# The output bias moves from GpSimd to VectorE and to a late place; the scatters of rows are no longer tied to TensorE's progress

## The chip, the cores and the metric

One core of one Trainium2 chip. The metric is the device time of one execution in microseconds (us), lower is better; before the change it is the median of three runs.

## The reference, cut to what matters

```python
x = L0_attn_x                               # (4, 512, 256) float32
xn = _layernorm(x, axis=-1)
# attention: 16 query heads of 16, one key/value head, window of 64, rotary on 8 of 16 dims
out = softmax(rope(q) . rope(k) * scale + mask) @ v
attn = out @ Wo + bo                        # bo: the output bias, one row of 256
# mixture of experts: 64 experts, 4 per token, 64 hidden, and two shared experts of 256
comb = top-4 gates of softmax(flat @ router_w), chosen with router_bias
routed = einsum('ne,nef,efd->nd', comb, silu(flat @ wg) * (flat @ wu), wd)
shared = sum over s of (silu(flat @ swg[s]) * (flat @ swu[s])) @ swd[s]
return x + attn + routed + shared
```

## The kernel before

The 2048 tokens are 16 tiles (NT) of 128; four tiles make one of the four batches (TPB = 4, B = 4). All five engines run hand-written streams side by side and meet at semaphores. On each engine the order in which the program issues is the order of execution.

**Start.** x is loaded (`x_in`, in the upper part of the tile `wall`), normalised into `x_n` (tile `spare`), turned on TensorE into `xnT`, and projected. The router runs on VectorE as a generator `routing()` whose steps are put between other work; it yields `slot_i`, for each token and each of its four experts the row of the DRAM buffer `xs_d` where its copy has to go (semaphore `slots`, L1229, once for tiles 0 to 7 and once for 8 to 15).

**Attention, 16 turns.** Turn T of every engine handles several tiles at different steps: TensorE computes the maxima of the scores of tile T (L459), the scores of T-1 (L487), the weighted values of T-1 (L530), the output projection of T-2 (L555). VectorE reduces the maxima (L1109), makes the parts of the float32 queries that bf16 leaves over (`leave`, L1103, two operands in SBUF), splits the maxima (L1118, L1120) and lays out the keys (`near`, L1095); `add_x` (L1154) adds x to the projected attention and SyncE stores the result in `base_d`.

**GpSimd in these turns.** `rotate(T)` applies the rotary embedding to the queries of a tile in four instructions (L1501 to L1507). `scatter()` issues 64 indirect DMAs (L1517, one for each tile and expert place), each writing 128 rows of 1 KB into `xs_d`. `add_bias(b)` (L1574) adds `bo` to the four tiles of `x_in` of batch b, so that `add_x` brings the bias along; it was loaded as one of the first DMAs into `bo_sb`. The order on GpSimd is: rotations 0 to 4 and the keys, the eight additions of batches 0 and 1, then a loop over T (L1597) that issues `SCATTERED_AT(T)` scatters, four or six, each after a wait for a product of TensorE in turn T, and after each of them one instruction of `rotate(T + 4)` or of `add_bias`.

**The blocks of experts.** When all 64 scatters have landed, SyncE loads blocks of 128 sorted rows (`xrow`, L1732), TensorE turns them (L639), and 32 groups (NGRP) of up to four blocks run: gate and up product (L665), `silu` on ScalarE (L913), the product of both on VectorE (`hidden`, L1301), the down product (L690), the copies out (L925, L1308) and the store to `y_d`. For each block GpSimd copies the weights of the expert that the router chose out of the resident tables (`pick_weights`, L1544, and `pick_down`, L1563). In groups 24 to 27 SyncE loads `base_d` back into `acc` (L1812, one DMA for each batch).

**The end.** The shared experts (L604, L889, L1315, L1319, L624), `add_shared` (L1326) into `acc`, and `sum_up` (L1341), which adds the four gathered rows of each token with their gates; GpSimd gathers them with 64 indirect DMAs (L1634).

## Time and profile before

| | |
|---|---|
| median of 3 runs | 394.87 us (392.55 to 395.25) |
| the profiled execution | 395.41 us, of which the span from first to last instruction is 394.1 us |
| TensorE busy | 345.3 us (88%) |
| GpSimd busy | 259.9 us (66%) |
| VectorE busy | 250.0 us (63%) |
| ScalarE busy | 189.1 us (48%) |
| mean granted TensorE clock | 0.961 of full speed |

Busy shares are means over stages with different limits: the start (to about 34 us), the attention (to about 172 us), the groups of experts (to about 290 us) and the shared experts with the sums (to the end).

### The profile page before, as it was taken

What the parts mean: (1) busy time and instruction counts of PE and PEld (TensorE: products, weight loads), DVE (VectorE), ACT (ScalarE), POOL (GpSimd) and SP (SyncE); (2) the same over time, 40 slices, a digit from 0 to 9 for tenths busy, and PEclk for the clock granted to TensorE, in tenths of its full rate; (3) what the DMA queues carried; (4) which work ended last, traced back from release to release, by engine and by line L of the source; (5) the groups of instructions that cost most, each with busy time, mean ns of one, the idle gap of its engine ahead of it and who ended that gap; (6) DMA issues with size and microseconds to landing.
All of it is one profiled execution on the core that took longest, in us unless ns stands there. A gap on an engine that the chain in (4) does not pass through costs nothing.

```text
span 394.1 us, 8678 instructions
## 1 busy us (share of the span) xinstructions
PE 345.3 (88%) x2710; PEld 254.8 (65%) x2711; DVE 250.0 (63%) x717; ACT 189.1 (48%) x359; POOL 259.9 (66%) x522
## 2 busy tenths in 40 slices
PE   6788597998888886999999999999999998899463
PEld 3676465666656554588999999999855544454352
DVE  4878797879889975555555544444443266581956
ACT  2684676788887873454555545545421010100100
POOL 5568988777687876326566667778647757575740
PEclk9999689899999998999999999999999999999958
DMA  8940245355665545779988845688753424343431
GB/s 253 220 122 3 81 129 158 123 163 162 175 182 166 187 150 162 198 215 292 298 258 268 258 146 176 205 279 277 270 180 105 118 80 133 90 142 90 119 108 40
DMA packets 73036, 66.81 MB, mean 170 GB/s; under 512 B 9053, under 2 KB 68701, under 8 KB 72993
## 3 DMA queue, kind: packets, MB, share of 16 engines
q1 hardware_dynamic: 66433, 49.30, 42.1%
q0 software_dynamic: 6144, 16.79, 13.6%
q8 instruction: 23, 0.38, 0.4%
q10 hardware_dynamic: 416, 0.18, 0.3%
q14 instruction: 20, 0.16, 0.1%
HBM read 36.78 MB, written 29.23 MB: 167 GB/s over the span
## 4 chain that ended last, share of the span: by engine, by line
PE 54%; DVE 18%; another core or an unknown queue 11%; issue 8%; ACT 7%; DMA 1%; POOL 1%; DVEq 0%; SPq 0%; ACTq 0%; POOLq 0%
PE bank L665 14%; PE bank L690 9%; PE bank L604 4%; PE bank L639 4%; DVE xall L1341 4%; PE bank L530 3%; PE bank L555 3%; PE bank L418 3%; DVE xall L1109 3%; PE bank L624 3%; PE bank L437 2%; PE bank L487 2%; ACT xall L855 2%; PE bank L406 2%
## 5 line engine op out<-in xcount | busy, mean ns | idle before, releaser
L1634 POOL DMA_INDIRECT wall<-y_d,y_row x64 | 60.9, 952 | 35.0 <-issue 18.3
L1517 POOL DMA_INDIRECT xs_d<-spare,slot_i x64 | 64.7, 1011 | 24.8 <-PE bank L487 6.3
L665 PE MATMUL bank<-xall,spare 128*128 x508 | 63.8, 278 | 0.0
L1301 DVE TENSOR_TENSOR spare<-bank,spare 64x512 f32<-64x512 f32 (+1 forms) x64 | 44.1, 689 | 31.0 <-ACT spare L913 30.2
L1544 POOL COPY spare<-wall 128x256 f32 x127 | 48.4, 400 | 19.4 <-PE bank L665 9.6
L665 PEld LDWEIGHTS bank<-xall,spare 128*128 128x128 f32 x508 | 59.4, 192 | 2.1
L604 PE MATMUL bank<-xnT,xall 128*128 128x512 f32 x128 | 58.3, 596 | 0.6 <-issue 0.3
L925 ACT ACTIVATE spare<-bank 128x512 f32<-128x512 f32 (+1 forms) x62 | 33.7, 593 | 27.9 <-PE bank L690 17.7
L624 PE MATMUL bank<-xall 128*128 128x256 f32 x128 | 33.2, 410 | 12.7 <-DVE xall L1326 8.7
L889 ACT ACTIVATE xall<-bank 128x512 f32<-128x512 f32 x16 | 9.2, 596 | 68.9 <-remote 51.6
L864 ACT ACTIVATE xall<-bank 98x1024 bf16<-98x1024 bf16 x32 | 32.7, 1023 | 19.9 <-PE bank L437 12.0
L604 PEld LDWEIGHTS bank<-xnT,xall 128*128 128x128 f32 x128 | 23.9, 190 | 26.9 <-issue 26.1
L624 PEld LDWEIGHTS bank<-xall 128*128 128x128 f32 x128 | 25.9, 206 | 23.6 <-DVE xall L1326 11.0
L872 ACT ACTIVATE xall<-bank 128x512 f32<-128x512 f32 x64 | 36.3, 600 | 7.5 <-PE bank L487 5.7
L1341 DVE SCALAR_TENSOR_TENSOR xall<-wall,gate,xall 128x256 f32<-128x256 f32 x64 | 31.0, 486 | 2.3
L913 ACT ACTIVATE spare<-bank 64x512 f32<-64x512 f32 (+1 forms) x32 | 18.8, 588 | 26.2 <-PE bank L665 26.1
L1109 DVE TENSOR_REDUCE xall<-bank 128x4 f32<-128x316 f32 x64 | 28.1, 477 | 2.4 <-remote 1.8
L855 ACT ACTIVATE xall<-xall 128x768 bf16<-128x768 f32 (+2 forms) x48 | 28.9, 626 | 1.1 <-DVE xall L1103 0.7
L1171 DVE COPY xall<-bank 128x256 f32<-128x256 f32 x32 | 13.6, 424 | 24.5 <-PE bank L639 24.1
L487 PE MATMUL bank<-xall,wdn 128*128 128x256 bf16 x120 | 21.9, 287 | 7.5 <-ACT xall L872 3.4
L1326 DVE TENSOR_TENSOR xall<-xall,bank 128x256 f32<-128x256 f32 x16 | 6.6, 417 | 25.8 <-remote 15.6
L1563 POOL COPY small<-wdn 128x128 f32 x24 | 7.0, 293 | 22.0 <-PE bank L690 21.3
(174 smaller groups left out, 648.8 us busy)
## 6 DMA issues: line engine op xcount, KB each, us to landing
y_d<-spare SPq DMA_DIRECT2D x31, 512.0 KB, 3.7
wall<-in_wg SPq DMA_DIRECT2D x16, 256.0 KB, 4.8
wall<-in_wu SPq DMA_DIRECT2D x16, 256.0 KB, 4.9
wdn<-in_wd SPq DMA_DIRECT2D x16, 256.0 KB, 4.4
spare<-xs_d SPq DMA_DIRECT2D x32, 128.0 KB, 2.9
small<-xs_d SPq DMA_DIRECT2D x32, 128.0 KB, 3.1
wall<-in_x SPq DMA_DIRECT2D x4, 512.0 KB, 5.6
base_d<-spare SPq DMA_DIRECT2D x16, 128.0 KB
```

What stands on the lines that cost most here:

```text
L604: ins = pe.matmul((gate_bank(i), up_bank(i))[half], wsh[:, c, half, ex, f0:f0 + P], xnT[:, c, g * GN:(g + 1) * GN], start=c == 0, stop=c = ...
L624: ins = pe.matmul(shared_bank(T), hs[T // GT % 2][:, k, t * P:(t + 1) * P], wshd[:, k, :], start=k == 0, stop=k == FC - 1)
L665: ins = pe.matmul(up_bank_of(G)[:, j * P:(j + 1) * P], wcur[i % NW][:, c * 2 * F:(c + 1) * 2 * F], x_half[c][:, bass.ds(o, P)], start=c == ...
L690: ins = pe.matmul(o[:, j * P:(j + 1) * P], hT[G % 2][rows64, j * P:(j + 1) * P], down_weights_of(G)[j][rows64, :], start=True, stop=True)
L855: act.activation(qt[:, :, first:first + n, :], source.unsqueeze(2).to_broadcast([P, H, n, HD]), ACT.Copy).then_inc(s["q_part"], 1)
L872: act.activation(probs[n % 2][:, e * 512:(e + 1) * 512], bank[2 + e][:, :], ACT.Exp).then_inc(s["exp"], 1)
L1109: dve.tensor_reduce(maxf[T % 2][:, w * 8 + 4 * e:w * 8 + 4 * e + 4], bank[e][:, 0:4 * NEAR].rearrange("p (g n) -> p g n", g=4), AX.X, ALU.max,
L1301: ins = dve.tensor_tensor(hT[G % 2][half, 0:n], up_bank_of(G)[F:P, 0:n], sg[0:F, 0:n], ALU.mult)
L1341: dve.scalar_tensor_tensor(a, yk[:, T, k, :], gate[:, T, k:k + 1], a, ALU.mult, ALU.add).then_inc(s["sum"], 1)
L1517: pool.indirect_dma_start(out=xs_d, out_offset=bass.IndirectOffsetOnAxis(ap=slot_i[:, T, k:k + 1], axis=0), in_=x_n[b][:, t, :], in_offset ...
L1544: pool.tensor_copy(wcur[i % NW].rearrange("p (c g f) -> p c g f", c=NC, g=2), wall[:, bass.ds(o, WE)].rearrange("p (g c f) -> p c g f", c= ...
L1634: pool.indirect_dma_start(out=yk[:, T, k, :], out_offset=None, in_=of, in_offset=bass.IndirectOffsetOnAxis(ap=y_row[:, T, k:k + 1], axis=0 ...
```

## The change

The bias is no longer added on GpSimd. VectorE adds it to `acc`, one instruction of 128 x 1024 elements for each batch, in groups 28 to 31, and `bo` is loaded in group 18. Later readers of `acc` wait for `with_bo`. On GpSimd the scatters wait for nothing but `slots`; turn 0 issues eight of them, turns 1, 12 and 13 five, the others four. Where no instruction of a rotation is there to stand between two scatters, a `memset` of 128 x 1 does. In `rotate`, the wait for the second instruction stands now behind the next scatter, in front of the third instruction.

```diff
+    bo_late = xrow[2]
-    SCATTERED_AT = lambda T: 6 if T in (NT - 4, NT - 3) else 4
+    BIAS_AT = 18
+    SCATTERED_AT = lambda T: 8 if T == 0 else 5 if T in (1, NT - 4, NT - 3) else 4
...
         def add_x(T):
             dve.wait_ge(s["attended"], T + 1)
-            dve.wait_ge(s["x_bo"], T + 1)
...
+        def add_bias(b):                       # VectorE
+            dve.wait_ge(s["bo"], 16)
+            dve.wait_ge(s[f"acc{b}"], 16)
+            a = acc[:, b * TPB:(b + 1) * TPB, :]
+            dve.tensor_tensor(a, a, bo_late.unsqueeze(1).to_broadcast([P, TPB, D]), ALU.add).then_inc(s["with_bo"], 1)
...
         for G in range(1, NGRP + 1):           # VectorE, the groups
             ...
             for b in turns_of(G)[1][:1]:
                 turn(b)
+            if NGRP - B <= G < NGRP:
+                add_bias(G - (NGRP - B))
...
         def scatter():                         # GpSimd
             for T in range(NT):
-                pool.wait_ge(s["slots"], T // (NT // 2) + 1)
+                if T % (NT // 2) == 0:
+                    pool.wait_ge(s["slots"], T // (NT // 2) + 1)
...
-        add_bias_whole(0)
-        add_bias_whole(1)
+        def apart():
+            if apart_n[0]:
+                pool.wait_ge(s["apart"], apart_n[0])
+            pool.memset(between[:, :], 0.0).then_inc(s["apart"], 1)
+            apart_n[0] += 1
         slots = scatter()
         for T in range(NT):
-            if T == 0:
-                pieces = add_bias(2)
-                for i in range(SCATTERED_AT(T)):
-                    next(slots)
-                    next(pieces)
-            else:
-                if T < NT - TPB:
-                    pieces = rotate(T + TPB)
-                elif T == NT - TPB:
-                    pieces = add_bias(B - 1)
-                for i in range(SCATTERED_AT(T)):
-                    if i < 2:
-                        pool.wait_ge(s["by_query"], PER_T * T + 2 * i + 2)
-                    elif i == 2:
-                        pool.wait_ge(s["by_key"], PER_T * (T - 1) + 3)
-                    else:
-                        pool.wait_ge(s["weighted"], QB * (T - 1) + min(i, 4) - 2)
-                    next(slots, None)
-                    if T < NT - TPB or i in (0, 4):
-                        next(pieces, None)
+            pieces = rotate(T + TPB) if 0 < T < NT - TPB else iter(())
+            for i in range(SCATTERED_AT(T)):
+                if next(slots, False) is False:
+                    break
+                if next(pieces, False) is False:
+                    apart()
+            for _ in pieces:
+                pass
         for _ in slots:
-            pass
+            apart()
...
-        sp.dma_start(bo_sb, bo.partition_broadcast(P)).then_inc(s["bo"], 16)     # SyncE, near its start
...
+            if G == BIAS_AT:                   # SyncE, in the groups
+                sp.wait_ge(s["g_T"], XB)
+                sp.dma_start(bo_late, bo.partition_broadcast(P)).then_inc(s["bo"], 16)
```

## Rows read from the trace of the kernel before

**Rows 1.** Busy time by stretch: start:end, length, each engine (instructions), clock, DMA.

```profile
120.00:140.00 20.00, 17.24 (x184) 10.95 (x181) 17.89 (x67) 17.12 (x30) 15.26 (x21) 1.00 0.54 165
```

**Rows 2.** Chain of waits, 38 to 43 us: start, length, engine, tile, line.

```profile
38.55 0.88 DVE xall L1103
...
41.34 0.77 DVE slot_i L1229
42.11 0.83 DVE wdn L1095
```

**Rows 3.** Timeline of GpSimd: start, busy, line, operation, tiles [idle before].

```profile
38.43 5.77 POOL L1574 TENSOR_TENSOR wall<-wall,wdn 128x256 f32<-128x256 f32 x8
...
58.94 0.98 POOL L1517 DMA_INDIRECT xs_d<-spare,slot_i  x1 [0.17 <-POOL xall L1507]
...
65.30 0.98 POOL L1517 DMA_INDIRECT xs_d<-spare,slot_i  x1 [0.17 <-POOL xall L1507]
...
158.16 0.96 POOL L1517 DMA_INDIRECT xs_d<-spare,slot_i  x1 [1.68 <-PE bank L530]
165.26 1.42 POOL L1544 COPY spare<-wall 128x256 f32 x4 [6.15 <-PE bank L510]
```

**Rows 4.** VectorE, the same instructions undisturbed: two of the timeline, one of the groups.

```profile
46.74 0.42 DVE L1103 TENSOR_TENSOR xall<-xall 128x256 f32<-128x256 f32 x1 [2.39 <-ACT xall L855]
...
60.54 0.35 DVE L1095 COPY wdn<-xall 98x640 bf16<-98x640 bf16 x1
...
L1252 DVE SCALAR_TENSOR_TENSOR y_row<-wdn 128x64 int32<-128x64 f32 x1 | 0.2, 227 | 0.0
```

**Rows 5.** Timeline around turn 13: the additions and VectorE's instructions.

```profile
141.73 0.70 DVE L1103 TENSOR_TENSOR xall<-xall 128x256 f32<-128x256 f32 x1
...
144.58 0.73 POOL L1574 TENSOR_TENSOR wall<-wall,wdn 128x256 f32<-128x256 f32 x1
144.63 0.98 DVE L1103 TENSOR_TENSOR xall<-xall 128x256 f32<-128x256 f32 x1
```

**Rows 6.** TensorE: one stretch by busy time, three rows of its timeline.

```profile
44.00:52.00 8.00, 6.76 (x33) 4.31 (x31) 5.39 (x19) 4.23 (x7) 7.22 (x9) 0.50 0.16 58
...
42.99 0.71 PE L459 MATMUL bank<-wdn,xall 128*128 128x79 bf16 x8 [2.60 <-DVE wdn L1095]
...
43.50 2.06 PE L418 MATMUL bank<-xall,xnT 128*128 128x256 f32 x4
...
55.91 1.10 PE L418 MATMUL bank<-xall,xnT 128*128 128x256 f32 x4
```

**Rows 7.** Who waited for whom, 40 to 160 us, GpSimd: sum, times, longest.

```profile
POOL xs_d L1517 <- PE bank L487: 6.3, 6, 1.2
```

**Rows 8.** Timeline of SyncE's queue and TensorE, where the attention ends.

```profile
161.87 1.74 SPq L1732 DMA_DIRECT2D spare<-xs_d  x4
...
166.44 0.63 PE L639 MATMUL bank<-cf,spare 128*128 128x128 f32 x4
```

**Rows 9.** Timeline of VectorE, turn 14.

```profile
149.08 0.69 DVE L1135 COPY xall<-bank 128x512 f32<-128x512 f32 x1 [2.32 <-PE bank L530]
...
152.00 0.49 DVE L1109 TENSOR_REDUCE xall<-bank 128x4 f32<-128x316 f32 x1 [1.53 <-remote]
```

**Rows 10.** An addition of 128 x 1024 on VectorE, and GpSimd under it.

```profile
69.62 1.23 DVE L1247 TENSOR_TENSOR wdn<-wdn,small 128x1024 f32<-128x1024 f32 x1
...
69.81 1.20 POOL L1505 TENSOR_TENSOR xall<-xall 128x64 f32<-128x64 f32 x1
```

**Rows 11.** Timeline, groups 28 to 30: VectorE, GpSimd, TensorE, and SyncE's last base load.

```profile
278.91 1.40 DVE L1301 TENSOR_TENSOR spare<-bank,spare 64x512 f32<-64x512 f32 x2 [1.68 <-ACT spare L913]
...
277.99 1.43 POOL L1544 COPY spare<-wall 128x256 f32 x4 [0.77 <-PE bank L665]
...
279.27 2.05 PE L665 MATMUL bank<-xall,spare 128*128 x16
...
275.60 0.51 SPq L1812 DMA_DIRECT2D xall<-base_d  x1
```

More of the change, by code:

```diff
@@ L116 @@
     "stats moments var scaled rs normed biased route member totals_read rank_read slots rows "
-    "q_left diag wslice shifted gate k_out k_near o_out max mpart max_out rden a_tok ah hs h y_out_dve gT_dve expert_read with_x based sum "
-    "v_fill fill prep roped k_split weights down_weights x_bo "
+    "q_left diag wslice shifted gate k_out k_near o_out max mpart max_out rden a_tok ah hs h y_out_dve gT_dve expert_read with_x with_bo based sum "
+    "v_fill fill prep apart roped k_split weights down_weights "
 ).split() + [f"fetched{T}" for T in range(NT - 1)] + [f"last_fetched{k}" for k in range(TOPK)]
@@ L173, in build @@
     unread = sb("unread", [P, 1])
+    between = sb("between", [P, 1])
     base_d = nc.dram_tensor("base_d", (NT, P, D), f32, kind="Internal").ap()
@@ L250, in build @@
     near_of = lambda T: 0 if T % TPB == 0 else 1 + (T - T // TPB - 1) % 2
-    bo_sb = rt.take(D)
     same = rt.take(NT * TOPK * TOPK).rearrange("p (t k i) -> p t k i", k=TOPK, i=TOPK)
@@ L325, in build @@
     route_at = lambda T: ROUTE[T] if T < len(ROUTE) else (0, 0, 2 - T % 2 if T < 12 else 1)
-    EXPERT_ROW, EXPONENTS = 13, 4
-    SCATTERED_AT = lambda T: 6 if T in (NT - 4, NT - 3) else 4
+    EXPERT_ROW, EXPONENTS, BIAS_AT = 13, 4, 18
+    SCATTERED_AT = lambda T: 8 if T == 0 else 5 if T in (1, NT - 4, NT - 3) else 4
     NORM = ((0,), (1,), (2, 3))
@@ L1319, in shared_hidden @@
             dve.scalar_tensor_tensor(hs[g % 2][:, k, :], ah[i % 2], 0.5, up_bank(i), ALU.mult, ALU.mult).then_inc(s["hs"], 1)
+        def add_bias(b):
[3 more added lines that the diff above has]
+            dve.tensor_tensor(a, a, bo_late.unsqueeze(1).to_broadcast([P, TPB, D]), ALU.add).then_inc(s["with_bo"], 1)
         def add_shared(T):
-            dve.wait_ge(s[f"acc{T // TPB}"], 16)
+            dve.wait_ge(s["with_bo"], T // TPB + 1)
             if T in SUM_FIRST:
@@ L1330, in sum_up @@
             if T in SUM_FIRST:
-                dve.wait_ge(s[f"acc{T // TPB}"], 16)
+                dve.wait_ge(s["with_bo"], T // TPB + 1)
             else:
@@ L1502, in rotate @@
             yield
-            prep(pool.tensor_tensor(rope[1], x12, over(k32["sin"]), ALU.mult))
+            prep_n[0] += 1
+            made = prep_n[0]
+            pool.tensor_tensor(rope[1], x12, over(k32["sin"]), ALU.mult).then_inc(s["prep"], 1)
             yield
+            pool.wait_ge(s["prep"], made)
             pool.tensor_tensor(x12[:, :, 0], rope[0][:, :, 0], rope[1][:, :, 1], ALU.subtract)
@@ L1518, in scatter @@
                                             in_=x_n[b][:, t, :], in_offset=None).then_inc(s["scattered"], 16)
-                    yield
+                    yield T
         expert_reg, down_reg = [[[ctx.enter_context(pool.register(f"{what}{n}_{i}")) for i in range(GS)] for n in range(2)]
@@ L1567, in gpsimd @@
         pool.wait_ge(s["c32"], 16)
-        def add_bias(b):
-            pool.wait_ge(s["bo"], 16)
-            pool.wait_ge(s["normed"], (b + 1) * TPB // 2)
-            pool.wait_ge(s["normed_act"], (b + 1) * TPB // 2)
-            for t in range(TPB):
-                pool.tensor_tensor(x_in[b][:, t, :], x_in[b][:, t, :], bo_sb, ALU.add).then_inc(s["x_bo"], 1)
-                yield
-        def add_bias_whole(b):
-            for _ in add_bias(b):
-                pass
         def rotate_whole(T):
@@ L1593, in gpsimd @@
         rotate_whole(4)
[L1594 to L1595 removed]
+        apart_n = [0]
+        def apart():
[3 more added lines that the diff above has]
+            apart_n[0] += 1
         slots = scatter()
         for T in range(NT):
[L1599 to L1618 removed]
+            pieces = rotate(T + TPB) if 0 < T < NT - TPB else iter(())
[6 more added lines that the diff above has]
+                pass
         for _ in slots:
[L1620 removed]
+            apart()
         pick_weights(0)
```

1 line of the change is left out of this document (removed).

## The prediction

> **What bounds the kernel now.** I read the busy time by stretch first. In the middle of the attention VectorE is busy 17.89 of 20 us [rows 1], ScalarE 17.12 and TensorE 17.24: all three take part in a cycle of about 7.3 us a turn, VectorE the fullest. GpSimd is busy 15.26 us of the same 20 and does nothing in it that another engine waits for soon. Then I read the chain of waits. Between 38 and 43 us it runs on VectorE through a subtraction (L1103), the conversion that yields the first slots (L1229) and the layout of keys (L1095), and from there to TensorE's maxima of turn 1 [rows 2]. Last I laid the timelines of VectorE and GpSimd beside each other. The reader is to see that in exactly this stretch GpSimd runs eight additions of the bias without a pause, 38.43 to 44.2 us [rows 3], and that three VectorE instructions of the chain are about twice as long as elsewhere. After 172 us the chain is on TensorE's expert products; neither the bias nor the scatters are in it.
>
> **The bias leaves GpSimd.** It removes 16 additions. The eight in front cost 5.77 us of GpSimd [rows 3]; nobody waits for them there, since GpSimd's next work, the first scatter, could not have begun before the slots at 42.11 us [rows 2]. What they cost is VectorE's time. Its L1103 takes 0.88 us on the chain [rows 2] against 0.42 in a stretch with no addition [rows 4]: 0.46. L1095 takes 0.83 of the chain (0.91 in the timeline) against 0.35: 0.5. L1229 takes 0.77; no undisturbed one is in the trace (the second, later, also has an addition beside it), the nearest is another conversion to int32 of twice the size, 0.227 us [rows 4]: between 0 and 0.55, and I take 0.55, as the two beside it have both doubled. Together 0.46 + 0.5 + 0.55 = 1.5 us, with some 0.1 from an instruction just before: **1.6 us**, all on the chain, since TensorE stands still until L1095 is done [rows 6]. In the changed kernel GpSimd is empty from 38.5 to 42 us and then issues a scatter; the undisturbed L1095 of 0.35 us in rows 4 lies wholly under a scatter, so a scatter does not lengthen it.
>
> Eight more additions stand one by one between scatters, four in turn 0 and four from 134 to 151 us. Two of turn 13 fall on L1103: 0.70 and 0.98 us [rows 5] for 0.42, so 0.28 + 0.56. The first is before VectorE's reductions and goes in full; of the second some is hidden, because TensorE and ScalarE are busy with scores meanwhile. Another of 134 us costs 0.15, and one beside the splitting of maxima about 0.4. Bounds are 0.3 (only the first) and 1.4 (all): I take **0.9 us**. The waits for `x_bo` on VectorE never came last (no wait in the trace is put down to L1574), so their removal is worth nothing.
>
> The Trainium skill, "SBUF — State Buffer", section "Who interferes with whom", gives the rule for such pairs: a VectorE instruction with two SBUF inputs, and a copy in its two-port mode, share a port pair with GpSimd by an exclusive lock, and whichever issues second waits for the first to end. The rows agree for L1103 (0.98 us, of which 0.68 lie under the addition). By that rule the same lock speaks against the late additions, below.
>
> **The clock.** Behind the 2.60 us for which TensorE waits on L1095 its granted clock is 0.50 from 44 to 52 us, the lower of the two levels [rows 6]. The four products of L418 take 2.06 us there and 1.10 at the full clock. Two such projections and the scores between them lie on the chain: two times 0.9, and some 0.3 for the rest, 2.1 us. The wait before shrinks from 2.60 to 1.0 us by the sum above; later TensorE is idle 2.8 of 20 us, in gaps of about 1 us, at a clock of 1.00 [rows 1]. Whether it stays up is open: 0 and 2.1 are the bounds, and I take half, **1.0 us**.
>
> **The scatters.** Untied, they no longer wait for TensorE: that releases 6.3 us on the scores [rows 7] and some 10 on other products. A scatter with a rotation's instruction behind it takes (65.30 - 58.94) / 4 = 1.6 us when nothing holds it [rows 3], one with a memset about 1.3 (0.98, a gap of 0.17, the memset). From 42.1 us: eight of 1.3 give 52.5; turn 1 four of 1.6 and one of 1.3 give 60.2; ten turns of 6.4 give 124; eleven of 1.3 give 138.5. The rotations can keep this pace, for TensorE projects a tile seven turns ahead and GpSimd gains only one turn on it. So the last scatter is issued about 137 us instead of at 158.16 [rows 3]. What follows it? SyncE gets to the loads of sorted rows at 160.4 us, held by its own order (store of tile 12), and waits 1.4 us for the scatters [rows 8]; it would load at 160.4. TensorE turns the first block at 166.44, with no idle time before it, so the rows were there. GpSimd's first weights are copied at 165.26, and TensorE uses them at 172.7. Hence the 20 us are hidden: **0**. The cover is TensorE's own order at the end of the attention.
>
> The removed ties have a price too. Rotations now drift against VectorE's turn. They are 1.5 us of each 7.3 and read SBUF; about five VectorE instructions a turn can collide. By chance a fifth of them would, each for about 0.2 us, that is 0.2 us a turn; before, L1120 alone was held for 0.1 to 0.2 us in most turns. I take 0, with bounds of 1.5 us to either side over eleven turns. The memsets write only, and 128 x 1.
>
> **The late part.** The load of `bo` goes from SyncE's start to group 18, behind a wait long fulfilled (the last block is turned in group 14); 128 KB then, with 40 us to spare. The four additions on VectorE have two SBUF operands and 1024 elements: 1.23 us each [rows 10], 4.9 us. In groups 28 to 30 they stand between two `hidden` with 1.68 us idle [rows 11], so 0.45 us remain; the fourth delays the last copy of y by 0.1 us, which TensorE's 14 us of shared products cover. `acc3` is issued at 275.60 and read at 288.6. Behind a waiting addition stand `hidden` and with it the down product; each base load comes at least 4 us before. The lock bites here: under L1247 a GpSimd instruction of 0.33 us took 1.20 [rows 10]. An addition from 277.2 to 278.4 us pushes the copy of 277.99 back by 0.45, to an end of its first block at 278.85; TensorE needs it at 279.27 [rows 11]. The next fall on weights wanted over 1 us later. I take **0**; if the cover is gone, three additions of up to 1.2 us, 3.6 us, are the bound.
>
> **Sum.** 394.1 - 1.6 - 0.9 - 1.0 = 390.6 us of span, and with the 1.3 us around it 391.9 for an execution like the profiled one (395.41). The median is 0.54 lower than that one, so 391.4.
>
> **Rivals.**
> *More than that* (0.17). The clock stays up altogether, another 1.1 us, and the stall of turn 14 shrinks. VectorE starts L1135 1.5 us after its product is ready and L1109 again 1.53 us late, put down to something outside [rows 9]; two weight loads and four scatters are in flight then, and the scatters would be gone. Against it: the loads stay, and the cause may be another. Worth 0 to 3 us: 387.3 to 389.9 us.
> *It comes to nothing* (0.22). VectorE's time is won but the turn waits for ScalarE or TensorE, or collisions elsewhere eat it; the 0.85 us of L1095 at the lower clock stay. 393.5 to 396 us. For it: three engines at 17 of 20 us [rows 1].
> *The late additions hold the weights* (0.05). 1 to 3.6 us lost in groups 28 to 31, against 2.5 won: 393.5 to 396.5.
> *Slower: the untied rotations fall on VectorE's chain every turn* (0.06). The ties kept GpSimd's instructions in phase with the turn. If without them both L1103 wait as in rows 5 (0.56 each) in eleven turns, that is 12.3 us against 2.5 won, 404.7. It decides from 0.6 us a turn, (2.5 + 3.9) / 11. Against it: 1.5 of 7.3 us of rotations can't hit both often, and their pace of 6.4 us differs from the turn's, so no bad phase lasts.
>
> **How the numbers follow.** The forecast has 0.50 and its own range 390.3 to 392.4 (2.5 to 4.6 won). 1% of 394.87 is 3.9 us, about what a measurement of this kernel can tell from no change: faster means below 390.9. That is the first rival whole and somewhat under half of the forecast: 0.38. Slower, above 398.8, is the last rival: 0.06. Same: 0.56. The range runs from 388.3, leaving out the lower third of the first rival, to 395.5, leaving out the last rival and the upper part of the middle two.
>
> **What would show it.** L1103, L1229 and L1095 between 38 and 42 us at 0.42, about 0.25 and 0.35 us; TensorE's wait before turn 1's maxima near 1 us and the clock from 44 to 52 us above 0.50; the last L1517 near 137 us; first L1732 at most 1.4 us earlier relative to turn 15; four additions of 1.2 us with TensorE's period of 3.07 us unbroken. It is wrong if turns 4 to 11 become longer than 7.5 us, if TensorE waits for L1544 in groups 29 to 31, or if turns 12 to 14 are as long as before.

## The result

The changed kernel is slower: **427.93 us** (median of 4 executions, 425.79 to 432.96) against 395.06 us of the kernel before in the same rounds (392.55 to 400.88), a ratio of 1.084 with a 95% interval of 1.075 to 1.093. (The ratio leaves out the slowest execution of each kernel; now and then an execution of any kernel runs one or two per cent longer.) The forecast was 391.4 us with a range up to 395.5. The profiled execution has a span of 427.6 us against 394.1.

One fact has to stand ahead of everything else: how much the change costs depends on the chip. The kernel before takes 391 to 395 us on some chips (**the first kind** below; the result above comes from one) and 371 to 374 us on others (**the second kind**). On the first kind the change costs 28 to 33 us. On the second the same changed kernel is 1.9 to 2.2% *faster* than the kernel before (ratios 0.981 and 0.978; the intervals reach from 0.970 to 0.985, so the gain is real, its size near 2%). No chip is known to have been used in two sets of runs. That it is the chip, and not something around it at the time, is therefore the simplest reading, and not shown.

### The profile after

Busy time by stretch (start:end, length, TensorE, its weight loads, VectorE, ScalarE, GpSimd, granted clock, DMA share, GB/s), kernel after:

```profile
40.00:60.00 20.00, 9.80 (x99) 6.84 (x96) 9.83 (x43) 10.35 (x17) 14.56 (x25) 0.92 0.38 126
60.00:80.00 20.00, 10.13 (x66) 6.34 (x67) 7.48 (x31) 5.87 (x11) 17.46 (x27) 0.65 0.30 97
...
140.00:160.00 20.00, 11.38 (x90) 6.76 (x94) 8.33 (x40) 8.67 (x16) 8.48 (x16) 0.60 0.29 93
160.00:180.00 20.00, 17.91 (x195) 11.68 (x188) 17.70 (x63) 17.38 (x29) 0.00 (x0) 1.00 0.37 103
```

Before, the middle of the attention had 17 to 18 of 20 us on three engines [rows 1]. Now there are two holes. From 50 to 80 us the three are busy 29 to 45% of the time and GpSimd 88%; from 132 to 159 us they are busy 45 to 60%. GpSimd issues its last scatter at 148.75 us; the old pace is back with the turn that begins at 159.00.

SyncE's stores of the maxima's parts, one pair a turn, give the turns (start, length, line): first the kernel before, then after.

```profile
39.59 1.22 SPq L1718 DMA_DIRECT2D xall<-xall  x2
...
52.00 1.15 SPq L1718 DMA_DIRECT2D xall<-xall  x2
...
58.84 1.15 SPq L1718 DMA_DIRECT2D xall<-xall  x2
```

```profile
41.22 1.22 SPq L1711 DMA_DIRECT2D xall<-xall  x2
...
50.19 1.26 SPq L1711 DMA_DIRECT2D xall<-xall  x2
...
74.82 1.15 SPq L1711 DMA_DIRECT2D xall<-xall  x2
...
159.00 1.20 SPq L1711 DMA_DIRECT2D xall<-xall  x2
...
166.06 1.21 SPq L1711 DMA_DIRECT2D xall<-xall  x2
```

The first turn shows the forecast at work: 8.97 us instead of 12.41, 3.4 won, counted from the first store, which this execution reaches 1.6 us later than the kernel before. The next takes 24.6 instead of 6.8. At the end of the attention the changed kernel is 30.9 us late (187.04 against 156.13 for the last such store), and the shared experts begin 29.4 us late (311.69 against 282.34); the remaining 4 us go in the last stage. So nearly all of the loss lies in the attention.

What stands in the first hole, timeline of TensorE, ScalarE, VectorE and GpSimd (start, busy, line, tiles [idle before <- what ended it]), kernel after:

```profile
50.91 1.07 PE L531 MATMUL bank<-xall 128*32 128x256 f32 x16
58.13 0.69 PE L460 MATMUL bank<-wdn,xall 128*128 128x79 bf16 x8 [6.15 <-issue]
...
65.22 1.09 PE L539 MATMUL bank<-cf,xall 128*128 128x128 f32 x4 [5.53 <-issue]
...
57.01 1.02 ACT L865 ACTIVATE xall<-bank 98x1024 bf16<-98x1024 bf16 x1 [5.86 <-remote]
...
69.25 1.02 ACT L865 ACTIVATE xall<-bank 98x1024 bf16<-98x1024 bf16 x1 [10.18 <-remote]
...
64.16 0.69 DVE L1136 COPY xall<-bank 128x512 f32<-128x512 f32 x1 [12.37 <-remote]
...
44.04 1.19 POOL L1529 DMA_INDIRECT xs_d<-spare,slot_i  x1 [3.48 <-DVE slot_i L1229]
...
54.39 0.96 POOL L1529 DMA_INDIRECT xs_d<-spare,slot_i  x1 [0.19 <-issue]
...
65.07 1.01 POOL L1529 DMA_INDIRECT xs_d<-spare,slot_i  x1 [0.17 <-issue]
```

TensorE's weighted values (L531) are over at 51.98 us. VectorE's copy of them (L1136) begins at 64.16, 12 us later, and the profile finds nobody on this core who released it: "remote". ScalarE waits in the same way for the turned queries. TensorE itself then stands still for what these two owe it. Meanwhile GpSimd issues a scatter every 1.27 to 1.6 us without a break from 44 us on. Between 40 and 165 us the changed kernel has 30.6 us of such waits at L865 (eight, the longest 10.2) and 16.7 at L1136 (two, the longest 12.4). Before, there were 6.7 us in the whole stretch: one wait of 4.9 us at ScalarE's L864 and two at VectorE's L1109, one of them that of [rows 9].

The same thing stood in the trace of the **kernel before**, in its last stage, where GpSimd issues gathers back to back:

```profile
310.29 3.60 PE L604 MATMUL bank<-xnT,xall 128*128 128x512 f32 x8
...
318.22 1.09 ACT L889 ACTIVATE xall<-bank 128x512 f32<-128x512 f32 x2 [14.03 <-remote]
...
313.82 0.94 POOL L1634 DMA_INDIRECT wall<-y_d,y_row  x1 [0.30 <-issue]
318.46 0.94 POOL L1634 DMA_INDIRECT wall<-y_d,y_row  x1 [3.70 <-remote]
```

ScalarE idles 14 us for products of TensorE that by the trace were done, until GpSimd itself comes to a wait and its train stops. The five waits of L889 there add up to 51.6 us. These rows were to be had before the forecast, and it didn't read them.

### The profile page after: what moved, and what is told of

Its sections match the earlier page's. It is cut to its first block, busy times and chain, and to the rows that moved or that the text cites. A ratio compares the mean times of both kernels' runs of the same rounds, so it can differ in the third digit from the quotient of the medians.

```text
span 427.6 us, 8657 instructions
## 1 busy us (share of the span) xinstructions
PE 353.7 (83%) x2710; PEld 261.2 (61%) x2711; DVE 251.8 (59%) x721; ACT 189.9 (44%) x359; POOL 252.2 (59%) x526
## 4 chain that ended last, share of the span: by engine, by line
PE 60%; DVE 13%; another core or an unknown queue 11%; issue 8%; ACT 6%; POOL 1%; DVEq 0%; ACTq 0%; POOLq 0%
PE bank L666 14%; PE bank L605 8%; PE bank L691 8%; PE bank L625 5%; PE bank L640 4%; PE bank L556 4%; PE bank L531 3%; DVE xall L1110 3%; DVE xall L1347 3%; PE bank L419 2%; PE bank L438 2%; PE bank L488 2%; PE bank L407 2%; ACT xall L873 1%
## 5 line engine op out<-in xcount | busy, mean ns | idle before, releaser
L1556 POOL COPY spare<-wall 128x256 f32 x127 | 50.1, 416 | 56.2 <-issue 40.3
L1529 POOL DMA_INDIRECT xs_d<-spare,slot_i x64 | 63.6, 993 | 14.2 <-issue 9.8
L666 PE MATMUL bank<-xall,spare 128*128 x508 | 63.8, 278 | 0.0
L865 ACT ACTIVATE xall<-bank 98x1024 bf16<-98x1024 bf16 x32 | 32.7, 1022 | 41.0 <-remote 30.6
L625 PE MATMUL bank<-xall 128*128 128x256 f32 x128 | 35.8, 435 | 15.1 <-DVE xall L1332 11.7
L625 PEld LDWEIGHTS bank<-xall 128*128 128x128 f32 x128 | 27.8, 219 | 25.9 <-DVE xall L1332 13.3
L890 ACT ACTIVATE xall<-bank 128x512 f32<-128x512 f32 x16 | 9.3, 596 | 69.3 <-PE bank L605 33.8
L488 PE MATMUL bank<-xall,wdn 128*128 128x256 bf16 x120 | 22.2, 290 | 12.2 <-ACT xall L873 9.3
L1136 DVE COPY xall<-bank 128x512 f32<-128x512 f32 x16 | 11.0, 690 | 30.2 <-remote 16.7
L460 PE MATMUL bank<-wdn,xall 128*128 128x79 bf16 x256 | 17.5, 211 | 11.6 <-issue 7.9
```

What stands on the lines that cost most here:

```text
L625: ins = pe.matmul(shared_bank(T), hs[T // GT % 2][:, k, t * P:(t + 1) * P], wshd[:, k, :], start=k == 0, stop=k == FC - 1)
L666: ins = pe.matmul(up_bank_of(G)[:, j * P:(j + 1) * P], wcur[i % NW][:, c * 2 * F:(c + 1) * 2 * F], x_half[c][:, bass.ds(o, P)], start=c == ...
L1529: pool.indirect_dma_start(out=xs_d, out_offset=bass.IndirectOffsetOnAxis(ap=slot_i[:, T, k:k + 1], axis=0), in_=x_n[b][:, t, :], in_offset ...
L1556: pool.tensor_copy(wcur[i % NW].rearrange("p (c g f) -> p c g f", c=NC, g=2), wall[:, bass.ds(o, WE)].rearrange("p (g c f) -> p c g f", c= ...
```

## The experiments

The theories that the expectations quoted below name by letters are explained in them as far as they are needed. The one that is left, D: where GpSimd issues indirect transfers in an unbroken train, what TensorE reports as done reaches the other engines late, on chips of the first kind alone; the four waits ("ties") that the change removes broke the train, since GpSimd itself waited for TensorE's reports. "Waits" in the tables is the sum of idle time ended by "remote" over all engines between 40 and 165 us; engines wait at the same time, so it is a sign and not a price (e13 below has 19.0 us of them and is faster than before).

### Second kind of chip: parts of the change

e1 is the kernel before with the late bias alone (ties kept). e2 is before without the ties:

```diff
                 for i in range(SCATTERED_AT(T)):
-                    if i < 2:
-                        pool.wait_ge(s["by_query"], PER_T * T + 2 * i + 2)
-                    elif i == 2:
-                        pool.wait_ge(s["by_key"], PER_T * (T - 1) + 3)
-                    else:
-                        pool.wait_ge(s["weighted"], QB * (T - 1) + min(i, 4) - 2)
                     next(slots, None)
```

e3 is the changed kernel with these six lines back from turn 1 on (`if T:`). e4 is the changed kernel with more memsets between the scatters, and tied to nothing:

```diff
                 if next(pieces, False) is False:
                     apart()
+                    apart()
+                apart()
...
         for _ in slots:
             apart()
+            apart()
+            apart()
```

> The kernel before with only the bias moved (late load in group 18, four additions on VectorE in groups 28 to 31, none on GpSimd); the ties of the scatters and their counts stay as before, and nothing stands where the additions stood. Theory A (the loss of 33 us comes from the untied train of indirect DMAs: while GpSimd issues them without a pause, TensorE's semaphore increments arrive late): 390 to 396 us, the 38 to 43 us stretch of VectorE 1.6 us shorter. Theory B (the late bias costs it: VectorE's additions or the late load): about 425 us, with TensorE waiting in groups 28 to 31. Theory C (GpSimd's additions in turn 0 were a needed pause between scatters): 400 us or more, with waits in turns 1 and 2.

> The kernel before with only the four waits of the scatters on TensorE's products taken away; the bias stays on GpSimd, the counts stay. Theory A: 415 to 435 us, VectorE and ScalarE waiting 4 us and more at a time for increments of TensorE (L530, L437) between 50 and 150 us, and only there. Theory B: 391 to 396 us. Theory C: about 400, as only turn 0 keeps its additions between the scatters.

> The changed kernel with the four waits put back in front of its scatters from turn 1 on; the memsets, the eight scatters of turn 0 and the late bias stay. Theory A: 390 to 400 us, a little over e1_late_bias for the burst of eight in turn 0. If the memsets or the burst of eight do the harm: above 410 us.

> The changed kernel without ties, but with more chained memsets after each scatter (three where no rotation stands, one behind each instruction of a rotation), so that the mean distance of scatters is near the 1.8 us of the kernel before. It tells whether the mean rate or the waiting on TensorE (which pauses GpSimd exactly when increments are late) keeps the kernel before healthy. Mean rate: 390 to 400 us. Waiting needed: 405 to 430 us, with fewer and shorter late increments than the 12 us of the changed kernel.

e7 is the changed kernel unaltered; e6 is e3 with a tie in the last stage:

```diff
             for k in range(TOPK - 1 if T < FETCH_FIRST else TOPK):
+                if T >= FC and k == 2:
+                    pool.wait_ge(s["projected"], T - FC + 1)
                 fetch(T, k, y_d)
```

> The changed kernel itself, on the chip of this set of runs. In the last set the kernel before took 371 us, not 395, and taking the ties away cost nothing. Theory D (the loss is a property of the chip: on some, TensorE's increments are late under a train of indirect DMAs): where the kernel before takes about 371 us, this takes 364 to 369; where it takes about 395, 420 to 435. Theory E (the loss belongs to the changed kernel's stream on any chip): 8% over the kernel before here too.

> e3_after_ties with one more wait for each tile in the gathers of the end: from tile 4 on, the third gather waits for the shared product of the tile four before. On a chip of the 395 us kind theory D expects the stage after the experts (104 us there, 87 us on the chip of the first set) to be 5 to 15 us shorter than e3's would be, so 375 to 390 us; on one of the 371 us kind no change from e3, 365 to 368 us.

| run | us | before beside it | ratio (95%) | waits |
|---|---|---|---|---|
| e1 late bias, ties kept | 366.72 | 371.03 | 0.987 (0.982 to 0.993) | none |
| e2 before without ties | 369.24 | 371.03 | 0.995 (0.992 to 0.998) | none |
| e3 after with ties | 366.23 | 371.03 | 0.986 (0.980 to 0.992) | none |
| e4 after, more memsets | 367.94 | 371.03 | 0.990 (0.984 to 0.995) | none |
| e6 e3 and a tie at the end | 367.24 | 373.68 | 0.982 (0.976 to 0.988) | none |
| e7 the changed kernel | 365.67 | 373.68 | 0.978 (0.970 to 0.985) | none |

All chips here were of the second kind. Every variant is at or a little under the kernel before (only the intervals of e6 and e7 reach to 2% and beyond), and no idle time in any of these traces ends with "remote", in the last stage neither. That e7, the very kernel of the result, is 8.0 us faster than before shows that none of its instructions is slow in itself. What follows is about the first kind.

### First kind: which part costs the time

The same kernels, unaltered, on chips of the first kind: e8 is the changed kernel, e9 is e3, e12 is e2, e13 is e1, and e14 is e6.

> The changed kernel once more, unaltered, to find out which kind of chip this is: where the kernel before takes about 395 us (as beside the result) or about 371 us (as beside e1 to e7). Theory D (late semaphore increments of TensorE under trains of GpSimd's indirect transfers belong to the chip): where before takes 395 us, this takes 420 us or more, with waits of 5 to 12 us of ACT's L865 and DVE's L1136 behind TensorE between 50 and 75 us; where before takes 371 us, 364 to 369 us with none. Theory E (the result was an accident of those executions, not of the chip): 364 to 369 us whatever before takes, or 0.98 of it.

> The changed kernel with the four waits of the scatters put back from turn 1 on (e3 again, unaltered). Theory D: where before takes 395 us, about 1 to 3% under it (385 to 393 us) with no wait of over 5 us behind TensorE before 150 us, some 35 us less than the changed kernel; where before takes 371 us, 365 to 367 us, the same as the changed kernel. A rival on a 395 us chip, that the late additions of the bias or the early start of the scatters cost the time: 420 us or more with the waits too.

> The kernel before without the four waits, nothing else changed (e2 again, unaltered). Where before takes 371 us: 367 to 370 us. Where before takes 390 us or more: if the lost ties are what cost the time, 410 us or more, with a turn of over 12 us behind a wait of over 5 us for TensorE; if it is the scatters' earlier start, 389 to 396 us.

> The kernel before with the late bias alone, the four waits kept (e1 again, unaltered). Where before takes 371 us: 366 to 368 us. Where before takes 390 us or more: 385 to 390 us if the ties, which it keeps, are what holds the increments' lateness off; over 395 us if the early start (here tied) costs it.

> The changed kernel with the four waits back from turn 1 on, and a wait of each tile's third gather for the product of the tile four before it (e6 again, unaltered). Where before takes 371 us: 365 to 368 us. Where before takes 390 us or more: about e9's 396 us less up to 10 us if pauses of the gathers let TensorE's increments through in the last stage; 394 to 398 us if that stage is bound by something else.

The last column is the time in the trace at which the shared experts begin, that is, the loss up to the last stage.

| run (one execution each) | us | before beside it | difference | waits | shared experts |
|---|---|---|---|---|---|
| the result (medians) | 427.93 | 395.06 | +32.9 | 63.8 | 311.7 |
| e8 the changed kernel | 418.93 | 390.53 | +28.4 | 59.8 | 307.0 |
| e9 after with ties | 396.39 | 390.53 | +5.9 | 23.0 | 284.1 |
| e12 before without ties | 402.74 | 391.3 | +11.4 | 28.6 | 292.0 |
| e13 late bias, ties kept | 388.28 | 391.3 | -3.0 | 19.0 | 277.9 |
| e14 e9 and a tie at the end | 394.18 | 391.3 | +2.9 | 26.4 | 284.0 |
| the kernel before | | | | 6.7 | 282.3 |

These are single executions, and on chips of this kind those of the kernel before spread over 6.5 and 8.3 us where there were several. So 28.4 and 22.5 us are clear of the noise, 11.4 is a little over it, and differences of 9 us and less are not shown by the times alone. The last column says more: e9 and e14, on two chips and the same up to there, differ by 0.1 us in it.

Theory E (an accident of the first measurement) falls: e8 loses 28 us again. The ties alone make 22.5 us of it (e8 against e9; 22.9 in the last column), and taken from the kernel before, which has additions between its scatters, they cost 11.4 (e12). The late bias looks 3.0 us faster here too (e13; 4.4 in the last column). Between e13 and e9 lie 8.9 us (6.2 in the last column): e9 issues eight scatters with a memset between them in turn 0, where e13 issues four before it meets its first tie; that this is the reason is read from the traces and was not tried by itself. The expectations for e9 (385 to 393) and e12 (410 or more) gave the early start too little and the ties of the kernel before too much.

The waits of e9, ties from turn 1 on (engine, tile, line, waited for: sum, times, longest; 40 to 165 us), and two rows of its timeline:

```profile
ACT xall L865 <- remote: 11.2, 3, 5.2
DVE xall L1136 <- remote: 9.4, 1, 9.4
...
51.84 1.02 ACT L865 ACTIVATE xall<-bank 98x1024 bf16<-98x1024 bf16 x1 [2.94 <-remote]
...
58.94 0.69 DVE L1136 COPY xall<-bank 128x512 f32<-128x512 f32 x1 [9.40 <-remote]
```

The long waits come at the end of a train of eleven scatters without a stop, 41.8 to 56.3 us: the eight of turn 0, and three of turn 1 whose ties were long fulfilled. After 60 us none is over 3.1 us. In e12, which starts with scatters 2 us apart (an addition between each two), nothing is late before 112 us, and then it comes:

```profile
134.63 0.69 DVE L1135 COPY xall<-bank 128x512 f32<-128x512 f32 x1 [5.39 <-remote]
...
138.30 1.02 ACT L864 ACTIVATE xall<-bank 98x1024 bf16<-98x1024 bf16 x1 [7.70 <-remote]
```

e14's extra tie in the last stage was meant to break the gathers' train and didn't: it held GpSimd for 0.3 us in all. So it tests nothing, and nothing changes that one execution can tell: from the first shared product to the end it takes 108.9 us, e9 111.0, e13 109.1; the changed kernel on a chip of the second kind (e18) 94.3. So on the first kind every variant loses 15 us or more in the last stage, the kernel before too (111.8).

### The lateness alone

e5 is a kernel of its own: a ring in which TensorE multiplies once, VectorE copies the product, ScalarE copies it again, and TensorE goes on, 24 rounds in each of eight phases of other work. e10 is the same on the first kind. e11 has trains of 40 transfers instead of 16, and more work of TensorE in a round:

```diff
                 if n:
                     pe.wait_ge(s["ac"], n)
+                if PHASES[p][1] == "dense":
+                    for _ in range(4):
+                        pe.matmul(other[:, 0:P], w[:, :], w[:, :], start=True, stop=True).then_inc(s["extra"], 1)
+                elif PHASES[p][1] == "long":
+                    for k in range(8):
+                        pe.matmul(other[:, :], w32[:, :], m32[:, :], start=k == 0, stop=k == 7)
                 pe.matmul(psum[:, 0:P], w[:, :], t2[:, :], start=True, stop=True).then_inc(s["mm"], 1)
```

> Not the computation: it writes zeros. A ring TensorE to VectorE to ScalarE to TensorE of one small instruction each goes round 24 times in each of eight phases, while GpSimd does nothing, 16 indirect scatters, 16 plain DMAs, nothing (16 DMAs from SyncE), 16 scatters with 1 us between, 16 indirect gathers, only memsets, and 16 scatters again. On a chip of the 371 us kind theory D expects about 1 us a round in all eight; on one of the 395 us kind the rounds under the unpaused scatters and gathers are several us, and only the step from TensorE to VectorE is late. If plain DMAs do the same, the cause is GpSimd's descriptor work; if SyncE's do, it is the traffic.

> The ring TensorE to VectorE to ScalarE of e5, one instruction each, 24 rounds in each of eight phases: quiet, under 16 scatters of GpSimd, 16 plain transfers of GpSimd, 16 of SyncE, scatters paused, gathers, memsets, scatters; it computes none of the reference and writes zeros. Theory D: where before takes 395 us, single rounds of the phases with unbroken indirect transfers last 2 us or more, the quiet phase and the memsets' 1.01 us; where before takes 371 us, 1.01 us in every round. If the rounds stay at 1.01 us on a 395 us chip, one engine's increment under scatters is not enough to make the lateness, and more of the kernel's load is needed for it.

> The ring TensorE to VectorE to ScalarE again, with trains of 40 indirect transfers of GpSimd, and in each round either one product, four more products that each add to a semaphore (dense), or eight more f32 products of 512 columns (long); phases: quiet dense, scatters with one, scatters dense, gathers dense, scatters dense with a pause after every fourth, quiet long, gathers long, and scatters dense with transfers of SyncE beside them. It computes none of the reference and writes zeros. Theory D2 (increments of TensorE are passed on at about one in 0.75 us under such a train): where before takes 390 us or more, a dense round under scatters or gathers lasts 3 us or more against under 2 in quiet, with the pauses less; a round with one product stays at 1.01 us. Theory D3 (it is the length of the train, not the number of increments): rounds with one product get longer too, after the first 8 us of the train. A rival: no round differs from quiet by over 0.2 us, and the lateness needs something else of the kernel. Where before takes 371 us, none of the rounds differs.

e5 (second kind) and e10 (first kind, 219.85 us) have 1.01 us in every round of every phase, the first round of a phase apart. A train of 16, 20 us long, with one report of TensorE in each microsecond makes nothing late, on the first kind neither. e11 (586.4 us, before beside it 391.3) does. VectorE in the phase of scatters with five reports a round; the train runs from 98.3 to 148.5 us, a quiet round takes 1.44 us:

```profile
107.36 0.29 DVE L57 CAST t<-bank 128x128 bf16<-128x128 f32 x1 [1.15 <-ACT t L62]
109.52 0.29 DVE L57 CAST t<-bank 128x128 bf16<-128x128 f32 x1 [1.87 <-PE bank L49]
...
124.27 0.29 DVE L57 CAST t<-bank 128x128 bf16<-128x128 f32 x1 [6.71 <-remote]
135.47 0.29 DVE L57 CAST t<-bank 128x128 bf16<-128x128 f32 x1 [10.91 <-remote]
148.77 0.29 DVE L57 CAST t<-bank 128x128 bf16<-128x128 f32 x1 [13.01 <-remote]
154.41 0.29 DVE L57 CAST t<-bank 128x128 bf16<-128x128 f32 x1 [5.34 <-remote]
155.85 0.29 DVE L57 CAST t<-bank 128x128 bf16<-128x128 f32 x1 [1.15 <-PE bank L49]
```

TensorE and ScalarE in the same phase, TensorE in the phase with pauses, GpSimd there:

```profile
136.16 0.61 PE L45 MATMUL other<-w 128*128 128x128 bf16 x4 [10.49 <-issue]
136.56 0.31 PE L49 MATMUL bank<-t,w 128*128 128x128 bf16 x1
...
135.79 0.31 ACT L62 ACTIVATE t<-t 128x128 bf16<-128x128 bf16 x1 [10.89 <-issue]
...
269.43 0.61 PE L45 MATMUL other<-w 128*128 128x128 bf16 x4 [0.73 <-issue]
...
267.85 0.96 POOL L83 DMA_INDIRECT ys_d<-rows,where  x1 [0.30 <-issue]
268.81 0.96 POOL L91 MEMSET waste<- 128x1024 f32 x1
270.06 0.96 POOL L83 DMA_INDIRECT ys_d<-rows,where  x1 [0.28 <-POOL waste L91]
```

The other two hops of the ring stay quick: VectorE's copy ends at 135.76 and ScalarE's begins at 135.79, that ends at 136.10 and TensorE begins at 136.16. The product is recorded from 136.56 to 136.87; VectorE can begin at 148.77. The 12 us lie behind TensorE alone (the trace models the end of a product, it doesn't record it). They grow while the train lasts, from its tenth microsecond on, up to 13.3 us for one round, and are gone 6 us after its end. The other phases of the same run: with one report a round, rounds stay at 1.01 us for the first 28 us of the train and then take 2.1 to 3.5. Under gathers it is as under scatters (up to 13.3 us). With eight long products a round, 7.9 us in quiet, one round takes 28.7. With SyncE's transfers beside the scatters it is no worse (up to 11.2 us). With a pause of 1.25 us after every fourth transfer all 32 rounds stay at 1.44.

So D2 (a fixed rate of one report in 0.75 us) falls, as five a round pass in 1.44 us for the first 10 us; D3 (the train's length alone) falls too, as five a round are late three times as early as one. Both the length of the train and the number of reports count, as they would in a backlog that fills. Where it is can't be seen in the trace, nor whether the report is late or the product itself ends later than its modelled end. Three things were not tried: e11 on a chip of the second kind (that the lateness is missing there is known from the kernels alone), a long train of plain transfers (those of e10 are 16, issued in 9 us), and a train as slow as the paused one but even (one transfer in 1.51 us against 1.26). Against the mere rate speaks the hole of the result's trace: with rotations between them its scatters are 1.5 us apart from 56 to 65 us, and the waits of 10 and 12 us are there.

### Pauses instead of ties

If breaking the train is all that the ties do, a pause of fixed length should do as well. e15 is the changed kernel with `pause()` after the fifth scatter of turn 0, after each turn's scatters and after every fourth of those left at the end; e16 has it after every eighth gather of the last stage as well:

```diff
+        def pause():
+            for _ in range(4):
+                apart()
+            pool.wait_ge(s["apart"], apart_n[0])
...
+                if T == 0 and i == 4:
+                    pause()
...
             for _ in pieces:
                 pass
+            pause()
...
                 fetch(T, k, y_d)
+            if T % 2:
+                pause()
```

> The changed kernel, its scatters tied to nothing, with a pause of GpSimd of about 1.3 us (four memsets of one column, each waiting for the one before) after the fifth scatter of turn 0 and after the four or five scatters of every turn. Where the kernel before takes 390 us or more: if the ties' work is to break the train of transfers, as the ring of e11 says, about as before or 1% under it (385 to 393 us), 30 us under the changed kernel's 419, with no wait for TensorE of over 5 us before 150 us. If it matters that GpSimd waits for TensorE itself, 405 us or more. Where before takes 371 us: 364 to 368 us.

> e15 with the same pause also after every eighth gather of the last stage. Where before takes 390 us or more: 375 to 385 us, 5 to 12 us under e15, with no wait for TensorE of over 5 us in the last stage, if trains of eight are short enough; as e15 if the last stage's late increments have another cause. Where before takes 371 us: 366 to 372 us, as GpSimd then needs 90 us for a stage in which TensorE needs 87.

Measured on a chip of the first kind, four executions each: e15 402.89 us, 1.022 of before (1.010 to 1.035); e16 403.06, 1.021 (1.013 to 1.028). The executions of e15 spread from 398.44 to 409.21; the two quicker ones are 5.3 us over the kernel before. Waits 25.3 and 24.0 us. Of e15:

```profile
55.18 1.02 ACT L865 ACTIVATE xall<-bank 98x1024 bf16<-98x1024 bf16 x1 [3.48 <-remote]
...
150.51 1.02 ACT L865 ACTIVATE xall<-bank 98x1024 bf16<-98x1024 bf16 x1 [4.96 <-remote]
```

The pauses take back some 20 of the 28 us that e8 loses (+5 to +9 instead of +28.4, on another chip), which supports the cause. They don't reach the 385 to 393 us expected. Whether ties do better than pauses is not settled: the whole times (+5.9 in e9) don't tell them apart, but the shared experts begin at 287.2 and 289.0 us in e15 and e16, and at 284.1 and 284.0 with ties (e9, e14). In the last stage the pauses bring nothing: the longest wait of L890 falls from 12.2 to 9.3 us, but the stage takes 114.5 us instead of 109.9 (e15's profiled execution was its quickest, e16's its slowest, so the difference itself says little). That 1.2 us after every eighth gather is enough there was wrong. The remedy that works in the attention has not been shown to work in the last stage, where the same waits stand; the loss of that stage stays open.

### The version that keeps the ties

e17 is e1 and e13 once more, e18 the changed kernel, side by side on one chip.

> The kernel before with the late bias alone, the four waits kept (e1 and e13, unaltered). Where the kernel before takes 390 us or more: 0.985 to 0.997 of it, with no wait for TensorE of over 5 us before 135 us. Where it takes 371 us: 0.983 to 0.992. If the late bias itself had a part in the loss there, over 1.01 where before takes 390 us.

> The changed kernel, unaltered. Where the kernel before takes 390 us or more: 1.06 to 1.09 of it. Where it takes 371 us: 0.975 to 0.985 of it. If the loss were an accident of the two calls that showed it, 0.98 to 1.0 also where before takes 390 us.

The chip was of the second kind (before 372.24 us): e17 368.30 us, 0.991 (0.988 to 0.994), e18 365.02, 0.981 (0.978 to 0.985). In e18, by stretch and on GpSimd's timeline:

```profile
40.00:60.00 20.00, 15.47 (x170) 11.18 (x170) 16.85 (x77) 16.74 (x28) 15.68 (x26) 1.00 0.43 137
60.00:80.00 20.00, 17.56 (x184) 11.94 (x182) 17.47 (x62) 17.68 (x33) 17.62 (x25) 1.00 0.57 184
...
137.69 0.96 POOL L1529 DMA_INDIRECT xs_d<-spare,slot_i  x1 [0.19 <-issue]
```

GpSimd's train is as dense as in the result's trace, and the three engines run at the old pace through it; no idle time ends with "remote". The late bias with the ties kept (e13: 388.28 against 391.3; e1 and e17: 0.987 and 0.991) is the one version that was not slower than before on either kind of chip. On the first kind that rests on a single execution, with a difference smaller than the spread.

## Why the prediction was wrong, point by point

**The step that failed** is "Untied, they no longer wait for TensorE: that releases 6.3 us on the scores". The forecast took the ties for a cost of GpSimd only, and priced their removal at the drift of the rotations: the term of "I take 0, with bounds of 1.5 us to either side". On chips like the one of the result the ties had a function that the code doesn't show: they stopped GpSimd again and again (27 waits, 16.8 us, between 40 and 160 us before), and without them what TensorE had done reached VectorE and ScalarE up to 12 us late. The term is 22.5 us (e8 against e9). None of the four rivals contained it. The slower one had the right place, untied GpSimd in the turns, but another mechanism (its instructions on L1103) and a third of the price. In the trace after, L1104 is 0.41 to 0.55 us in the slow turn; that rival did not occur.

**Early scatters at 0** was probably the second miss: "the 20 us are hidden" looked only at who waits for the scatters, not at what the earlier and denser train does to others. With the ties kept e9 is 8.9 us over e13, 6.2 of them before the shared experts; each is a single execution.

**A sign not used.** The forecast read "1.53 <-remote" in turn 14 [rows 9] and gave it to "something outside". In the same trace ScalarE waited 14.03 us in the same way. Under the question "what does GpSimd do at the time?" both rows give the same answer: a train almost without a stop, nine scatters from 139 to 152 us with waits of at most 0.32 us between them, and gathers 1.25 us apart.

**The sign it named did come:** "turns 4 to 11 become longer than 7.5 us". In the trace after the seven turns between 89.44 and 159.00 us take 7.9 to 15.2 us.

**The bias leaves GpSimd: right.** VectorE's chain in the trace after, and TensorE behind it:

```profile
40.65 0.43 DVE L1104 TENSOR_TENSOR xall<-xall 128x256 f32<-128x256 f32 x1
...
42.97 0.18 DVE L1229 TENSOR_SCALAR slot_i<-wdn 128x32 int32<-128x32 f32 x1
43.07 0.32 DVE L1096 COPY wdn<-xall 98x640 bf16<-98x640 bf16 x1
...
43.44 0.47 PE L460 MATMUL bank<-wdn,xall 128*128 128x79 bf16 x8 [1.43 <-DVE wdn L1096]
43.74 1.10 PE L419 MATMUL bank<-xall,xnT 128*128 128x256 f32 x4
...
67.87 2.06 PE L419 MATMUL bank<-xall,xnT 128*128 128x256 f32 x4
```

Against [rows 2]: 0.45, 0.59 and 0.51 us, together 1.55 where 1.5 was forecast; the value at the upper bound for L1229 was right. These are the rows of one execution each; e1 and e18 have the same 0.18 and 0.32 us. The rule of the Trainium skill ("SBUF — State Buffer", "Who interferes with whom") agrees: without the addition on GpSimd L1104 is 0.43 us. TensorE's wait shrank from 2.60 [rows 6] to 1.43, not to the 1.0 forecast.

**The clock: right in kind, more than valued.** From 44 to 52 us, where the forecast looked, the granted clock is 1.00 in the trace after instead of 0.50, and L419 takes 1.10 us instead of 2.06. (Other traces have 0.79 to 1.00 in this stretch with the bias late, and 0.71 and 0.79 with it on GpSimd, so part of the contrast is chance.) Of the 3.4 us by which that turn is shorter TensorE's wait is 1.2; the other 2.2 are as much as the forecast's upper bound for the clock, 2.1, of which it took half. The three terms of the sum, 3.5 us, are what e1 (4.3) and e17 (3.9) and, on the first kind, e13 (3.0) measure. In the holes the clock falls, to 0.65 of full speed from 60 to 80 us and 0.60 from 140 to 160, and a hole costs more than its waits: L419 takes 2.06 us at 67.87, as in [rows 6].

**The last scatter** was forecast for 137 us. It is issued at 137.69 in e18 and at 148.75 in the result, where GpSimd had to wait for TensorE's projections (10.3 us in five waits of L1509 for ScalarE's L832). "The rotations can keep this pace" holds only as long as the turns do.

**The late part at 0: right.** VectorE around the first of the four additions, kernel after:

```profile
305.19 1.40 DVE L1301 TENSOR_TENSOR spare<-bank,spare 64x512 f32<-64x512 f32 x2 [1.67 <-ACT spare L914]
306.62 1.41 DVE L1325 TENSOR_TENSOR xall<-xall,spare 128x1024 f32<-128x1024 f32 x1
308.26 1.40 DVE L1301 TENSOR_TENSOR spare<-bank,spare 64x512 f32<-64x512 f32 x2 [0.23 <-ACT spare L914]
```

The additions take 1.23 to 1.41 us and fall into VectorE's idle 1.67; the period stays 3.07 us. (Two slips of the working change nothing: by its own terms the first rival ends at 390.3 and not at 389.9, and the 0.85 us that the second rival gives to L1095 stands in no row.)

**On the second kind** the forecast would have been too small instead: 8.0 and 7.2 us won (e7, e18) against 3.5. Some 2 to 3 us more than the bias seem to come from the untied scatters (e2 1.8; e18 over e17 3.3; e7 over e6 1.6), the size of the rival "More than that". Where in the turns they lie was not settled: the profiled executions of e17 and e18 have the same span, 364.0 and 363.8 us.

## What to carry to other kernels

A wait that seems to hold only an idle engine may be what keeps that engine's work from making others late: before removing it, look for places in the trace where the engine already runs without pause, and for waits there with no releaser on the core. A change that makes a train of small transfers denser should be measured on more than one chip, as its sign can depend on it. Of two changes made together, take the one with the local and explained gain (here the bias, about 4 us on the second kind) by itself.

## What the runs showed of the hardware

- The same kernel takes 371 to 374 us on some chips (three of those used here) and 391 to 395 us on others (those of the result, e8, e12 and e15). From the first shared product to the end it is 111.8 us of the kernel before on a chip of the first kind, 94.3 of e18 on one of the second. From the last store of the attention to the first shared product it is 126.2 us in the kernel before and 125.9 in e17. What differs is not known, nor is it shown that it stays with a chip.
- On the first kind, what TensorE has done reaches VectorE or ScalarE up to 12 us late while GpSimd issues indirect transfers 1.26 us apart without a pause (e11: VectorE waits 13.01 us where 1.15 is usual, and with long products 28.4 where 7.6 is usual). It builds up in 10 us with five reports a round of 1.44 us, in 28 us with one in 1.01 us, and is gone within 6 us after the train. The hops from VectorE to ScalarE and from ScalarE to TensorE stay below 0.1 us.
- A pause of 1.25 us after every fourth transfer kept it away altogether in the ring (32 rounds of 1.44 us), and only in part in the kernel (e15).
